# Three more tables looked up by one-hot matmuls instead of gathers, in a one-core DLRM tower

## The reference

```python
e = jnp.stack([tbl_0[ids[:, 0]], ..., tbl_25[ids[:, 25]]], axis=1)     # 512 x 26 x 128
combined = jnp.concatenate([dense[:, None, :], e], axis=1)             # 512 x 27 x 128
interactions = jnp.einsum('bnd,bmd->bnm', combined, combined)          # 512 x 27 x 27
z = jnp.concatenate([dense, interactions[:, triu_i, triu_j]], axis=1)  # 351 pairs
h = jnp.concatenate([z, dense], axis=1)                                # 607 columns
h = jnp.maximum(h @ W_top1 + b_top1, 0.0)                              # 512
h = jnp.maximum(h @ W_top2 + b_top2, 0.0)                              # 256
y = h @ W_top3                                                         # 512 x 1
```

## Time and profile before

| | |
|---|---|
| time, median of three runs | 105.53 us (104.25 to 107.01) |
| profiled execution, first to last instruction | 141.4 us |
| PE matmul, busy | 105.4 us |
| PE weight load, busy | 85.9 us |
| DVE, ACT, POOL, busy | 52.7, 48.3, 60.9 us |
| DMA | 13.46 MB |

### The profile page before, as it was taken

One profiled execution on the slowest core, in us unless ns is written; L12 is line 12 of the kernel. 1 busy time (PEld: TensorE's weight loads), 2 busy tenths in 40 slices (PEclk: granted clock), 3 DMA queues, 4 the chain that ended last, 5 costly groups with the idle time before them and its releaser, 6 DMA issues.

```text
span 141.4 us, 3474 instructions
## 1 busy us (share of the span) xinstructions
PE 105.4 (75%) x1525; PEld 85.9 (61%) x1525; DVE 52.7 (37%) x116; ACT 48.3 (34%) x82; POOL 60.9 (43%) x66
## 2 busy tenths in 40 slices
PE   6999899999979960366795223441997999967993
PEld 2476678788858950164684122221996998957980
DVE  2999999699279800000050000000043034103210
ACT  4749929597079520201023000000105106310342
POOL 1887877478567775705227777770000000000000
PEclk9999999999999997558689555555599999998699
DMA  4899999999992122100101122220000000000000
GB/s 131 282 234 256 264 262 234 249 241 234 305 381 71 51 60 55 38 19 23 37 5 48 48 59 57 56 56 19 0 5 5 5 5 0 0 5 5 5 0 1
DMA packets 5365, 13.46 MB, mean 95 GB/s; under 512 B 1731, under 2 KB 1991, under 8 KB 5222
## 3 DMA queue, kind: packets, MB, share of 16 engines
q1 hardware_dynamic: 3260, 9.11, 24.1%
q0 software_dynamic: 1920, 3.94, 10.8%
q10 hardware_dynamic: 170, 0.18, 0.4%
HBM read 13.23 MB, written 0.00 MB: 94 GB/s over the span
## 4 chain that ended last, share of the span: by engine, by line
PE 65%; issue 23%; DVE 6%; ACT 2%; DMA 2%; DVEq 0%
PE ps_a L334 27%; PE ps_gram L371 11%; PE ps_a L420 9%; DVE onehot L560 5%; PE ps_h L434 5%; PE ps_rows L349 4%; PE ps_a L410 3%; PE ps_a L397 2%; DMA idrow<-ids_by_table 2%; PE ps_rows L447 1%; ACT xt L659 1%; DVE part_sb L569 1%; PE ps_h L460 1%; ACT table_sb L666 1%; PE ps_gram L390 0%
## 5 line engine op out<-in xcount | busy, mean ns | idle before, releaser
L307 POOL DMA_INDIRECT rows_sb<-tbl,ids_sb x60 | 60.5, 1009 | 34.1 <-issue 16.5
L334 PE MATMUL ps_a<-onehot,part_sb 125*128 125x512 f32 (+1 forms) x208 | 46.9, 376 | 2.9 <-issue 2.6
L334 PEld LDWEIGHTS ps_a<-onehot,part_sb 125*128 125x128 f32 x208 | 35.8, 197 | 11.2 <-issue 3.4
L371 PE MATMUL ps_gram<-xt 128*27 128x27 f32 x1024 | 16.9, 205 | 22.5 <-issue 21.6
L371 PEld LDWEIGHTS ps_gram<-xt 128*27 128x27 f32 x1024 | 13.5, 118 | 27.1 <-issue 25.1
L560 DVE TENSOR_SCALAR onehot<-idrow,row_id 125x1024 fp32r<-125x1024 int16 (+1 forms) x42 | 27.7, 712 | 4.9 <-remote 3.3
L608 DVE TENSOR_SCALAR table_sb<-ps_a,columns_sb 128x128 f32<-128x128 f32 x8 | 2.4, 347 | 43.7 <-PE ps_a L420 39.5
L420 PE MATMUL ps_a<-table_sb,w_sb 128*128 128x128 f32 x72 | 13.0, 326 | 6.8 <-issue 6.4
L652 ACT COPY xt<-ps_a 128x512 f32<-128x512 f32 (+1 forms) x13 | 7.5, 575 | 31.1 <-PE ps_a L334 18.9
L587 DVE STREAM_TRANSPOSE table_sb<-ps_gram 128x864 f32<-128x864 f32 x4 | 4.3, 1084 | 32.3 <-PE ps_gram L371 32.3
L420 PEld LDWEIGHTS ps_a<-table_sb,w_sb 128*128 128x128 f32 x72 | 11.2, 232 | 7.6 <-issue 6.9
(11 more groups left out here) (35 smaller groups left out, 46.0 us busy)
## 6 DMA issues: line engine op xcount, KB each, us to landing
table_sb<-tbl SPq DMA_DIRECT2D x11, 448.0 KB
idrow<-ids_by_table SPq DMA_DIRECT2D x5, 256.0 KB
w_sb<-w SPq DMA_DIRECT2D x1, 1280.0 KB, 8.7
rows_sb<-tbl,ids_sb POOLq DMA_INDIRECT x60
table_sb<-tbl SPq DMA_DIRECT2D x10, 52.0 KB
w_sb<-w SPq DMA_DIRECT2D x1, 512.0 KB
dense_sb<-dense_by_column SPq DMA_DIRECT2D x1, 256.0 KB
idrow<-ids_by_table ACTq DMA_DIRECT2D x1, 128.0 KB
```

The costliest lines, as they stand in the source:

```text
L307: pool.indirect_dma_start(rows_sb[:, t % ROWS_RING, k, :], None, tables[f], bass.IndirectOffsetOnAxis(ids_sb[:, t, f:f + 1], 0),).then_inc ...
L334: last = pe.matmul(ps_a[:, i % 2, a:b], parts_sb[part][:, w, c * D:(c + 1) * D], unit_onehot(u, c)[:, member, a:b], start=(part == HIGH an ...
L371: last = pe.matmul(ps_gram[j * NPAD:j * NPAD + N, half, s * N:(s + 1) * N], x, x, start=True, stop=True)
```

## The change

Tables 0, 1 and 5 (1250 rows) join the tables looked up on PE. They are cut into ten chunks of 125 rows and stand at places 7 to 9, each a unit of its own; the ring's slots and buffers grow to ten chunks where they were eight. Twelve tables are left to gather, in three groups of four for each tile: 48 gathers, 12 groups. Ten of the groups are turned after lookups 3 to 12 of the now 14 tables (12 full ones, two in halves), the last two after the lookups; none is turned between the layers of tiles 1 and 2 any more. The row numbers for ten chunks are made by two more iotas on POOL.

```diff
-ONEHOT_TABLES = [4, 10, 11, 17, 19, 20, 24, 25, 3, 8, 14]
+ONEHOT_TABLES = [4, 10, 11, 17, 19, 20, 24, 0, 1, 5, 25, 3, 8, 14]
 VP = 125
-CHUNKS = [8] * 11
+CHUNKS = [8] * 7 + [10] * 3 + [8] * 4
...
-UNITS = [[0], [1, 2], [3, 4], [5, 6], [7, 8], [9, 10]]
+UNITS = [[0], [1, 2], [3, 4], [5, 6], [7], [8], [9], [10, 11], [12, 13]]
...
-GROUP_SIZES = [4, 4, 4, 3]
+GROUP_SIZES = [4, 4, 4]
...
-AFTER_LOOKUP = [[], [], [], [0], [1], [2], [3], [4], [5], [6], [7]]
+AFTER_LOOKUP = [[], [], [], [0], [1], [2], [3], [4], [5], [6], [7], [8], [9], []]
...
-            turn_group(8)
+            turn_group(10)
             layer1_dense(0, 0)
             layer1_dense(0, 1)
             turn_z(0)
-            turn_group(9)
+            turn_group(11)
             gram(1, 0)
...
             layer1_dense(1, 1)
-            turn_group(10)
             turn_z(1)
-            turn_group(11)
 
             gram(2, 0)
...
             layer1_dense(2, 1)
-            turn_group(12)
             turn_z(2)
-            turn_group(13)
 
             for m in range(M1):
                 layer1_pairs(2, m)
-            turn_group(14)
             layer2(2, 0)
-            turn_group(15)
             layer1_dense(3, 0)
             gram(3, 0)
...
-            copy_group(8)
+            copy_group(10)
             copy_z(0)
-            copy_group(9)
+            copy_group(11)
             relu1_low(0)
             relu2(0)
-            copy_group(10)
             copy_z(1)
-            copy_group(11)
             relu1_low(1)
             relu2(1)
-            copy_group(12)
             copy_z(2)
-            copy_group(13)
             relu1_low(2)
-            copy_group(14)
-            copy_group(15)
             relu2(2)
```

## The result

The changed kernel takes 120.03 us (median of 4 runs, 119.13 to 120.62) against 105.75 us for the kernel before on the same chip (4 runs): 1.145 times as long, 95% interval 1.134 to 1.157. It is 14.3 us slower. Forecast were 118.7 us and a range of 110 to 122.

The account below looks back on a forecast made before the run. PE was taken to bound the kernel from the first lookup to the end. Matmuls +14.6, transposes +1.1 and borders -2.55 gave +13.2 us on 105.5: 118.7 us, range 110 to 122.

Parts of the forecast that it names:

- The pauses are not in the timed runs: PE's pauses beside gathers, 22.6 and 14.8 us, belong to the profiled execution; at most 1.5 to 3.6 us to timed ones.
- 60 x 0.244 = +14.6 us, all on PE's path: Three added ten-chunk lookups: 60 matmuls of 512 columns, one started every 0.244 us, add 14.6 us on PE.
- DVE at the ten-chunk tables: DVE's compares and low parts take 5.4 us a table against PE's 5.3: cost 0, bounds 0 and +2.1 us.
- Waits for gathered rows: Group 9, turned after lookup 12's first half, finds gather 39 landed: cost 0, to +1.5 us if POOL is behind.
- The engines moved 214 GB/s, so no wait: Ten-chunk lookups need 185 GB/s of tables, id rows and gathers; the engines moved 214 GB/s, so no wait.
- W1 and W2: Weight loads, issued when lookup 9 has both parts, some 25 us before the first layer: cost nothing.
- The borders, -2.55 us: Later stages lose transposes at three borders: -1.3 us tiles 1 to 2, -0.35 tiles 2 to 3, -0.9 before the last gram.
- rival A: A small part of the pauses, 1.5 to 3.6 us, is real and goes with late gathers: 115 to 117 us; chance 0.14.
- Rival B: Pauses beside gathers are the kernel's own in timed runs too; 22.6 us go, giving 96 us; chance 0.10.
- Rival C: DVE (+2.1 us) or gathers (+1.5 us) become the bound at the ten-chunk tables: 121 to 122.5 us; chance 0.10.
- D: PE starts matmuls faster where no records are written: 8.1 to 13.1 us for the 60, 112 to 117 us; chance 0.08.
- One sign of being wrong: PE idle before lookups 8 to 12 in the changed kernel's profile would show the prediction wrong.

Follow-up runs that it names:

- the second profile: The kernel before, unchanged, profiled once more: 104.1 us, span 102.3 us, at clock 1.0.
- the last experiment: The kernel before with layer 2's second half of tile 2 and the last dense part placed between quarters of the last gram: 106.62 us, ratio 1.012.

## Why the prediction was right, and where it was not

**The pauses are not in the timed runs.** Right, shown by the second profile and by the kernel without gathers. The step "104.0 us against 105.53" was off by little: the span is 102.3 us and 1.8 us lie around it. The reason given for it, that something follows behind the records of PE's instructions, is not shown; the second profile speaks against it.

**"60 x 0.244 = +14.6 us, all on PE's path."** The size is nearly right, 13.9 us. "All on PE's path" is half the truth. The lookups are bound by PE, but halving the new matmuls saves nothing with gathers and 0.3 us without them. Had the tables needed only their high parts, this step would have forecast 111.4 us against 120.2 measured.

**DVE at the ten-chunk tables, taken as 0.** Right for the kernel as it is: 5.03 us measured between units against 4.99 of PE (the prediction had 5.4 and 5.3), and without gathers no lookup waits for DVE. It is the bound that comes next.

**Waits for gathered rows, taken as 0 with a bound of +1.5 us.** This is the term that was mis-sized: 2.6 us as marked, 3.1 us on PE's path. For group 9, the only one that the prediction looked at, it was nearly right. Gather 39 landed 2.5 us after its issue (forecast 2.3), PE came 2.35 us after lookup 11's end (forecast 2.6), and POOL was late by half a gather; the wait of 0.84 us lies inside the bound and has the cause that the prediction gave for it. The step that failed is that no other group was asked about. Groups 6 and 7 waited 1.32 and 0.47 us, though their last gathers were allowed two lookups ahead. POOL issued gather 27 4.4 us after that, where "1.009 + 0.3 us for a gather" would have kept pace, and it took 6.8 us to land. From what the trace says of the gathered rows' tile, the kernel after (shortest, median and longest time from issue to landing):

```profile
DMA to landing us min/median/max: 2.5/7.2/9.0
```

With the weights loaded later neither group waited: gather 27 was issued 0.8 us earlier and landed in 5.7 us, gather 31, the last of group 7, landed in 2.7 us instead of 5.4. So both had a part, POOL's lateness and the queue. POOL waited for lookups for only 0.6 us in all; it was no longer ahead of PE. "The engines moved 214 GB/s, so no wait" was the wrong question: bandwidth left over says nothing of the queue in front of a gather.

**W1 and W2: "nothing".** Wrong in kind. They are in time for PE, but whatever is queued behind them is not; moved by some 12 us they cost 3.9 us in the comparable executions.

**The borders, -2.55 us.** Measured -1.2 (from the dense part to the gram 2.97 us before, 1.80 after; the rows stand above), -0.1 and -1.0: -2.3. The rest of the -3.4 us of that stretch is grams that run at 0.75 us for 64 records instead of up to 1.00. The kernel before without gathers runs them at 0.75 as well, so it is the gathers beside them. That is rival A, at 1 us and not 1.5 to 3.6.

**Not foreseen:** the last gram, +1.5 us in the profiled executions, since two pauses fall into it instead of one. It varies between executions; how much of it is in the medians is open.

**The sum.** +13.2 forecast, +14.3 measured: right by its main term. That the rest comes out small is luck. In the profiled executions the waits (+3.1) and the last gram (+1.5) stand against shorter grams 0 to 2 (-1.6) and slightly cheaper matmuls and transposes (-0.9), and none of these was in the sum. (The spans differ by 15.9 us, the medians by 14.3: the second profile of before is of an execution 1.4 us under its median.) One sign of being wrong that the prediction named did appear: PE idle before lookups 10 and 11.

**The rivals.** Rival B is refuted. Rival C happened in its second half (gathers), at twice the price given there. D has little for it: 512-column matmuls of the lookups are 0.23 us apart at full clock in all profiles, and the timed runs exceed their spans by the same 2.2 us as the profiled one; but no run without records is on hand. The spacing of 131 ns that the Trainium skill gives (TensorE: Matmul & The Clock Gate, Back-to-back issue gap) appears in no profile of this case.

## What to carry to other kernels

When a profiled execution is much longer than the timed ones, find one stretch that occurs twice in it, disturbed and undisturbed, and price the disturbance by the difference; then profile once more before explaining it. A share of work moved from a helper's queue to the engine that bounds costs its full length there, however long the helper's list was: count what the helper's idle end is worth first (here the removal of all gathers was worth 1 us). Read the landing time of a transfer where it will be issued: the 2.5 us of a gather behind idle DMA engines were 6.8 us beside the loads of tables and weights. Ask it of every group, not only of the one with the least slack. And when taking matmuls away saves nothing, look at the granted clock before naming the next bound.

## What the runs showed of the hardware

**A pause tied to the place in the program.** In the last gram PE starts a weight load and a matmul for 64 samples in 1.3 us. In every kernel with such a run of short instructions it pauses once or twice, for 0.4 to 2.7 us, with nothing to wait for. In the kernel after the pauses stand behind 102 and 230 matmuls of the gram (the rows above): 128 matmuls apart, 256 instructions. With twelve tables the pause of 1.62 us falls just behind the gram, into layer 2:

```profile
90.70 2.51 PE L371 MATMUL ps_gram<-xt 128*27 128x27 f32 x256
93.14 0.94 PE L434 MATMUL ps_h<-table_sb,w_sb 128*128 128x128 f32 x6
95.70 0.49 PE L434 MATMUL ps_h<-table_sb,w_sb 128*128 128x128 f32 x2 [1.62 <-issue]
```

The Trainium skill (Runtime: NRT & Kernel Launch, Instruction fetch mechanics) says that an engine's instructions are fetched in blocks of 256, and that the cost of crossing a block is mostly hidden. The distance agrees with the first half; where 256 instructions take 1.3 us, the second doesn't hold here. In the last experiment slower instructions among the 151 shortened the pause from 2.01 to 0.89 us, which fits too. That the pause is a fetch is argued, not shown.

**PE's clock falls behind idle stretches.** In the changed kernel with half the matmuls of its new tables the granted clock is 1.0, PE idles for 2.63 us, and then it is 0.5 for some 3 us; without gathers it falls during an idle 2.09 us, with the weights later during 4.83. At 0.5 the 512-column matmuls of the lookups are 0.44 us apart instead of 0.23. It isn't a matter of the last wait alone: behind the pause of 2.17 us in the kernel after, the clock stayed at 1.0.

**Gathers are slow to land behind full queues.** In the kernel after, the ten gathers issued from 23.5 to 37 us landed 8.2 us later in the median, with the DMA engines at a share of 1.0; the last nine, from 61.6 us on, took 2.5 us.

**Fewer gathers don't mean a faster POOL.** 48 gathers took 1.15 us each on the average, 60 had taken 1.01. Most of the long ones lie from 30 to 47 us, where DMA is full and DVE compares for one-table units; which of the two it is wasn't tried. Single ones took 5.1 us (with eight groups beside the lookups, and with weights in pieces).
